# Attention turn of a macaron block: maxima taken in pairs, router logits and norm statistics moved in VectorE's order

## The reference

```python
x = x + 0.5 * ffn(layernorm(x))     # 8 experts, each takes the T/8 tokens of highest router probability
x = x + attn(layernorm(x))
x = x + 0.5 * ffn(layernorm(x))

def attn(x):                        # 32 sequences of 512 rows, causal
    q, k, v = x @ W_q.T, x @ W_k.T, x @ W_v.T
    scores = where(causal, q @ k.T / sqrt(256), -inf)
    return (softmax(scores, -1) @ v) @ W_o.T
```

## Time and profile before

| | |
|---|---|
| median of 3 runs | 2369.24 us (2361.5 to 2376.99) |
| profiled execution, its time | 2374.09 us |
| its span, first to last instruction | 2372.4 us |
| mean granted TensorE clock | 0.918 |
| busy: PE, DVE, ACT, POOL | 83%, 59%, 61%, 59% |
| attention: first scores' maximum to last turn's | 1009.14 to 1480.36 us |
| DMA busy in attention, 1060 to 1450 us | 0.78 of the 16 DMA engines |

### The profile page before, as it was taken

One profiled execution on the slowest core, in us unless ns is written; L12 is line 12 of the kernel. 1 busy time (PEld: TensorE's weight loads), 2 busy tenths in 40 slices (PEclk: granted clock), 3 DMA queues, 4 the chain that ended last, 5 costly groups with the idle time before them and its releaser, 6 DMA issues. The chain is left out here.

```text
span 2372.4 us, 41314 instructions
## 1 busy us (share of the span) xinstructions
PE 1962.8 (83%) x14720; PEld 1333.8 (56%) x14720; DVE 1405.5 (59%) x4037; ACT 1445.2 (61%) x2800; POOL 1400.6 (59%) x1591
## 2 busy tenths in 40 slices
PE   4713899899999999499999999208899999999998
PEld 4611556566666666366666666104566666656665
DVE  6987654545454453277777777587545555454532
ACT  6944455556566566377777776345565656655654
POOL 6702575666666666567777774214666666666665
PEclk8555999999999999799999999558999999999999
DMA  8793354555454544468887775303455454546444
GB/s 287 283 319 82 85 99 81 89 103 96 79 116 80 92 77 59 89 128 172 175 169 170 178 166 137 100 19 99 98 84 100 93 89 87 93 83 110 69 65 45
DMA packets 423422, 275.58 MB, mean 116 GB/s; under 512 B 299056, under 2 KB 402480, under 8 KB 422960
## 3 DMA queue, kind: packets, MB, share of 16 engines
q1 hardware_dynamic: 365872, 205.65, 34.7%
q0 software_dynamic: 57344, 67.29, 18.9%
HBM read 120.76 MB, written 101.71 MB: 94 GB/s over the span
## 5 line engine op out<-in xcount | busy, mean ns | idle before, releaser
L1092 DVE SCALAR_TENSOR_TENSOR hid_l<-hf,hid_h 128x512 f16<-128x512 f32 x512 | 354.4, 697 | 528.6 <-ACT hid_h L616 375.0
L1270 PE MATMUL ps<-w_h,hid_l 128*128 128x256 f16 x2048 | 559.1, 273 | 8.9 <-issue 8.6
L1269 PE MATMUL ps<-w_l,hid_h 128*128 128x256 f16 x2048 | 559.0, 273 | 8.4 <-issue 8.2
L1268 PE MATMUL ps<-w_h,hid_h 128*128 128x256 f16 x2048 | 559.4, 273 | 7.6 <-issue 7.1
L702 ACT ACTIVATE hf<-ps,b 128x512 f32<-128x512 f32 x512 | 344.6, 673 | 217.2 <-remote 120.3
L1268 PE MATMUL ps<-xt,w_h 128*128 128x512 f16 x1024 | 399.8, 390 | 53.4 <-ACT hf L702 32.3
L540 POOL DMA_INDIRECT xe<-z_d,tok x256 | 270.5, 1056 | 255.9 <-DVE gate_at L1079 171.7
L1269 PE MATMUL ps<-xt,w_h 128*128 128x512 f16 x1024 | 399.8, 390 | 4.9 <-issue 4.9
L1270 PE MATMUL ps<-xt,w_l 128*128 128x512 f16 x1024 | 399.0, 390 | 3.0 <-issue 2.9
L616 ACT ACTIVATE ys<-yb,weight 128x256 f32<-128x256 f32 x256 | 128.1, 506 | 378.2 <-DVE yb L1110 317.5
L616 ACT ACTIVATE hid_h<-hf 128x512 f16<-128x512 f32 x512 | 322.4, 630 | 16.2
(11 more groups left out here) (259 smaller groups left out, 3910.5 us busy)
## 6 DMA issues: line engine op xcount, KB each, us to landing
w_st<-fc_t SPq DMA_DIRECT2D x32, 1024.0 KB
xin<-x SPq DMA_DIRECT2D x32, 512.0 KB, 5.4
z_d<-zz SPq DMA_DIRECT2D x32, 512.0 KB, 3.8
xin<-x_d SPq DMA_DIRECT2D x32, 512.0 KB, 4.5
out<-x SPq DMA_DIRECT2D x32, 512.0 KB, 5.3
z_d<-z SPq DMA_DIRECT2D x32, 512.0 KB, 3.3
xe<-z_d,tok POOLq DMA_INDIRECT x256, 3.2
xt<-xs SPq DMA_TRANSPOSE x256
```

The source lines that it names most:

```text
L1092: dve.scalar_tensor_tensor(hid_l[:, n % 2, f, :], hf[:, f % HF, :], HS, hid_h[:, n % 2, f, :], ALU.mult, ALU.subtract).then_inc(s_hl, 1)
L1268: pe.matmul(dst, lh, rh, start=first, stop=False)
L1269: pe.matmul(dst, lh, rl, start=False, stop=False)
L1270: return pe.matmul(dst, ll, rh, start=False, stop=last)
```

## The change

DVE's order inside the attention turn changes, and nothing else. `biases` now takes a pair of row blocks: two maxima, then one multiplication that writes both columns of `nbias` and raises `s_max` by 2. The router logits of sequence l move from behind the fourth maximum to ahead of the third. The second norm's statistics of sequence r move from between the second and the third maximum to behind the fourth.

```diff
-                def biases(q):
-                    dve.wait_ge(s_s, TG * a + (q + 1))
-                    if q == 0:
+                def biases(pair):
+                    if pair == 0:
                         wait(dve, s_prob, TG * a)
-                    link(dve.tensor_reduce(nmax[:, q:q + 1], bank(q)[:, 0:P * (q + 1)], AX.X, ALU.max, negate=True))
-                    dve.tensor_scalar(nbias[:, q:q + 1], nmax[:, q:q + 1], SCORE, None, ALU.mult).then_inc(s_max, 1)
+                    for q in (2 * pair, 2 * pair + 1):
+                        dve.wait_ge(s_s, TG * a + (q + 1))
+                        steps.done(dve.tensor_reduce(nmax[:, q:q + 1], bank(q)[:, 0:P * (q + 1)], AX.X, ALU.max, negate=True))
+                    steps.sync()
+                    both = slice(2 * pair, 2 * pair + 2)
+                    dve.tensor_scalar(nbias[:, both], nmax[:, both], SCORE, None, ALU.mult).then_inc(s_max, 2)
 
                 if on(a):
                     biases(0)
                     lo_half(s_vh, a, v_flat_l[:, v], v_flat_h[:, v], s_vl, 1)
+                if on(l):
+                    group_logits(l, 7, NG)
+                if on(a):
                     biases(1)
                 if on(r):
                     dve.wait_ge(s_x2, TG * (r + 1))
                     wait(dve, s_scale2, r - 1)
                     stats(x2[:, r % 2], 2 + r % 2).then_inc(s_mv2, 1)
-                if on(a):
-                    biases(2)
-                    biases(3)
-                if on(l):
-                    group_logits(l, 7, NG)
```

## The result

The changed kernel takes 2423.94 us (median of 4 runs, 2420.51 to 2428.17) against 2368.96 (4 runs, 2361.5 to 2376.99): 1.0239 times as long, 95% interval 1.0213 to 1.0265 (the ratios here and below are estimated from the single runs, and need not be the quotient of the two medians). It is 55 us slower; 6 us faster were forecast, and the range ended at 2372.

What follows compares the result with a forecast made beforehand. Two attention-turn cycles, one through PE, DVE and ACT, one through a DMA queue, were taken to bound it. 0.20 us a turn gives 5.6 us, plus 0.4 at start and end: 6.0 saved, 2363.2 us; range 2353 to 2372.

Steps and rivals of the forecast that it cites:

- Pair 1: DVE's maxima 2 and 3: maximum 3 starts 0.90 us earlier, exponent 2 0.11 earlier, `u_h` 0.33 earlier.
- Two multiplications fewer: On DVE: some 0.15 us a turn saved, in time now spent waiting for scores 3, so worth nothing.
- The slow rival: Statistics held up beside POOL's half of `z2r` start 1.56 us later; 28 turns cost 25 us, 2394; chance 0.06.
- cycle A: Attention turn's path PE scores, DVE, ACT, DVE, PE: 15.01 us a turn, to become 14.68.
- The rule against pairing: Skill's advice that breaking up Vector instructions may finish sooner; as rival, pairing holds exponent 2 back, 2380 us, chance 0.02.
- Cycle B: Two-turn path through the DMA queue, from `zc` to `z2c` transposes and logit products: 15.14 us a turn, to become 14.97.

Runs made afterwards that it cites:

- the kernel with the multiplications apart: The changed kernel with each pair's multiplication written as two of one column each; 2366.42 us against 2369.37 for the kernel before (0.9976).
- three columns: The changed kernel with each pair in a row of three columns, the third zero, and one multiplication taking all three; 2423.59 us.
- two inputs: The changed kernel with the pair's multiplication as a two-column tensor_tensor of two SBUF operands; 2406.31 us beside 2353.08 for the kernel before.
- half: The changed kernel with GpSimd's `z2r` subtraction covering two of four row blocks; 2365.45 us beside 2353.08 for the kernel before.
- pairing alone: The kernel before with only the maxima paired, statistics and logits in their old places; 2272.26 us against 2236.67 for the kernel before.

## Why the prediction was wrong

**The step that failed** is in *Pair 1*: "From its start to the exponent 0.91 pass". The 0.91 was read from a multiplication of one column and carried over to one of two columns that runs while GpSimd subtracts. There it is 1196.15 to 1198.63, 2.48: 1.57 more, and the forecast turn of 14.68 with 1.57 on top is 16.25, where 16.24 was measured. *Two multiplications fewer* priced the new form at "Nothing"; it cost 1.1 us a turn, net of what the moves give. The trace of before held no `tensor_scalar` of several columns beside the subtraction. The nearest row of such a form is in the residual, with 4 columns (32 times, 0.158 to 0.164 us), and three times it started beside the GpSimd instruction that did not hold the multiplication above either:

```profile
1473.43 0.16 DVE L1202 TENSOR_SCALAR rinv<-rsum 128x4 f32<-128x4 f32 x1
```

```profile
1472.99 1.01 POOL L500 TENSOR_TENSOR nt<-nt,minus_half 128x4 f32<-128x4 f32 x1
```

It was not held, so it would not have warned either. The new form beside the subtraction had no price in that trace. It should have been a rival of its own, with the rest of the subtraction as its bound.

**The slow rival had the mechanism and the wrong victim.** It let GpSimd's `z2r` subtraction hold up the statistics for 1.56 us, cycle A at 16.10. A hold exists and measured 1.47 (1.64 less the 0.17 of the same form when it is not held), with turns of 16.24. But it hit the multiplication ahead of the statistics. The rows against it were sound for the statistics, which in the kernel with the multiplications apart take 1.40 us beside the subtraction, and said nothing on another form. Its chance of 0.06 came from looking at the moved instructions and not at the rewritten one. It ended at 2394, 30 us short, of which the clock is 21.

**The clock** was in no case's price. The windows showed it full in the kernel before, where the idle time shown ahead of values 0 was 0.33; with 2.40 it fell in every second turn.

**What was right**, by the kernel with the multiplications apart: no wait for the logits, maximum 3 waiting for scores, exponent 3 0.57 behind exponent 2 (1197.68 to 1198.25), exponent 1 0.35 behind exponent 0, and cycle A at 14.67 to 14.71 (forecast 14.68). The size of the gain is not confirmed: 6.0 us were worked out, the medians differ by 2.95, the ratio gives 5.7 with an interval from 11.6 us less to 0.2 more, and the mean turn of 15.10 is 0.11 shorter than before where 0.20 were taken, 3.1 us in 28 turns (one turn of 17.03 is in it). The rule against pairing (breaking up instead) gave no loss there, but the single multiplications with both moves reach 14.52, so pairing still costs some 0.15 a turn without any hold.

**Cycle B** was argued and stays so. Its sum proves nothing: 15.43 + 14.84 is the distance of the two `zc` issues, 15.00, plus that of the two logit products, 15.27, and two such distances come to two turns whatever binds them. What speaks for it is that PE sits idle right ahead of the logit products in most of the longer turns, and not in the shortest, those of cycle A. Here is such a turn, of 15.48 us, in the kernel with the multiplications apart:

```profile
1147.53 0.17 PE L1303 MATMUL ps<-rw_h,z2c 128*128 128x8 f16 x1 [0.64 <-issue]
```

The view names no releaser for it; that it is the DMA of `z2c` follows only from what the products read. Turns between the short ones remain in every variant, and a changed order of issue does not free them. Whether the engines' bandwidth or SP's issue is what bounds them, these runs leave open.

## What to carry to other kernels

A VectorE instruction that becomes wider, even from one column to two, may start to wait for GpSimd: look at what GpSimd runs at that moment, and price the new form only from rows of that form beside that very instruction. Where a small SBUF-to-SBUF step stood on the path beside a long GpSimd subtraction, two multiplications of one column cost 0.04 us more than one of two (0.21 against 0.17) and did not wait. A stall that comes each turn can cost twice, as here, once by itself and once by the TensorE clock: read the granted clock in windows before and behind the longest idle time.

## What the runs showed of the hardware

- A `tensor_scalar` of 2 or 3 float32 columns, SBUF to SBUF, and a `tensor_tensor` of 2 columns with both inputs in SBUF, ended 0.02 to 0.03 us behind a running GpSimd subtraction of 512 or 1024 columns in all five kernels shown (changed, three columns, two inputs, half, pairing alone), whatever was left of it (0.5 to 1.6 us). One-column `tensor_scalar` never took over 0.156 us in the kernel before, 128 times, 60 of them beside that subtraction.
- GpSimd's power of two SBUF inputs (4 columns, 1.01 us) did not hold the 2-column `tensor_scalar`: 0.17 us in 12 turns.
- `BATCH_NORM_STATS2` kept its duration beside the subtraction (1.40 for four in the kernel with the multiplications apart, 1.39 without it in the changed one), and so did maxima read from PSUM (0.68 for 512 columns beside it in the kernel before, 0.69 ahead of it in the changed one).
- One idle time of 2.40 us in each turn of 16 us brought the granted TensorE clock down in every second turn, at a cost of 1.65 us each. The same turn length kept it full with idle times of 1.30 and 0.90 (pairing alone, on another chip), and with the gap filled by matmuls of no use.
